# A graph layer pair on one core: node rows load behind the small weights, the count's pieces come in a row, the second chunk's weights move a step forward, and the source key is counted in strided pieces

## What is computed

```python
h = jnp.maximum(_layernorm(x, axis=-1), 0.0)
hid = silu(edge_attr_16 @ (Wfc1 / 4.0))                 # per edge
w = hid @ (Wfc2 / 8.0)                                  # per edge, 192 values
e0, e1 = f0[src], f1[src]                               # features of the source node
mid = products of w, e0, e1 and edge_attr_4
n = segment_sum(mid, dst) / max(count(dst), 1)          # mean at the destination
x = x + (self connection of h) + alpha * (n @ Wl2)
```

## Time and profile before

| | us |
|---|---|
| median of 3 runs | 9377.47 (9372.29 to 9378.21) |
| the profiled execution | 9408.31 |
| its span, first to last instruction | 9406.5 |
| first scatter of the counting stage begins | 51.09 |
| last one ends | 2201.92 |

### The profile page before, as it was taken

How to read it: one execution, slowest core, us unless ns; L and a number is a source line. 1 busy time by engine, 2 the same in 40 slices (tenths; PEclk the granted TensorE clock), 3 DMA queues, 4 the chain that set the end, 5 groups by cost and what they waited for, 6 DMA issues and landing times. The chain is left out here.

```text
span 9406.5 us, 172851 instructions
## 1 busy us (share of the span) xinstructions
PE 6619.1 (70%) x31166; PEld 4409.1 (47%) x31166; DVE 7124.6 (76%) x21336; ACT 4949.5 (53%) x16490; POOL 6802.1 (72%) x6877
## 2 busy tenths in 40 slices
PE   6666665654655555556566556778799999999999
PEld 4333333332222222222222222356588888888888
DVE  7666666665777777777777778977799999999995
ACT  4444444443444444444444445644477777777774
POOL 6777777777777777777777776456677777777770
PEclk7655556666888888888888888989899999999999
DMA  3222222225666676666676666545556666666667
GB/s 110 91 92 92 92 91 92 91 90 164 215 214 212 215 213 212 214 210 215 211 215 210 215 212 206 181 145 173 157 164 169 169 168 169 169 169 166 169 166 229
DMA packets 1189746, 1589.22 MB, mean 169 GB/s; under 512 B 452520, under 2 KB 967336, under 8 KB 1189544
## 3 DMA queue, kind: packets, MB, share of 16 engines
q1 hardware_dynamic: 789336, 836.46, 28.9%
q0 software_dynamic: 328704, 651.74, 24.0%
q10 hardware_dynamic: 71632, 100.24, 3.0%
HBM read 999.62 MB, written 1050.39 MB: 218 GB/s over the span
## 5 line engine op out<-in xcount | busy, mean ns | idle before, releaser
L1693 PE MATMUL pair<-prod_m,hot_m 128*128 128x160 f32 x14848 | 2244.5, 304 | 165.4 <-DVE prod_m L1899 128.9
L1580 POOL DMA_INDIRECT feat_m<-feat_tab,rows_m x1856 | 1830.6, 986 | 580.0 <-issue 445.4
L1693 PEld LDWEIGHTS pair<-prod_m,hot_m 128*128 128x128 f32 x14848 | 2042.9, 190 | 367.1 <-issue 365.1
L1714 ACT ACTIVATE hot_m<-hot_m,rows_m 128x128 f32<-128x128 f32 x5568 | 1728.5, 389 | 701.0 <-DVE hot_m L1882 696.7
L1591 POOL DMA_INDIRECT fetched_m<-feat_tab,index_m x1664 | 1666.4, 1001 | 517.9 <-issue 500.3
L679 POOL DMA_INDIRECT sorted_rows<-rows_e,place_e x1664 | 1629.5, 979 | 531.1 <-issue 515.3
L1726 ACT ACTIVATE prod_m<-part_m,rows_m 128x64 f32<-128x64 f32 x5568 | 1432.4, 337 | 1008.6 <-DVE part_m L1919 835.7
L1608 POOL DMA_INDIRECT sorted_rows<-later_m,place_m x1248 | 1240.8, 994 | 523.4 <-issue 376.4
L1674 PE MATMUL bank<-prod_m,hot_m 128*128 128x449 f32 x2476 | 1120.4, 576 | 548.9 <-DVE prod_m L1939 336.8
L1899 DVE TENSOR_TENSOR prod_m<-rows_m,feat_m 128x192 f32<-128x192 f32 (+2 forms) x4640 | 1284.8, 309 | 0.0
L490 PE MATMUL pair<-fc,hT_m 64*128 64x224 f32 x2496 | 397.9, 447 | 963.9 <-ACT later_m L1769 960.0
(11 more groups left out here) (259 smaller groups left out, 10631.1 us busy)
## 6 DMA issues: line engine op xcount, KB each, us to landing
agg_tab<-acc_m ACTq DMA_DIRECT2D x928, 320.0 KB
rows_m<-sorted_rows SPq DMA_DIRECT2D x928, 229.0 KB
agg_tab<-acc_m ACTq DMA_DIRECT2D x928, 224.5 KB
rows_m<-sorted_rows SPq DMA_DIRECT2D x928, 197.0 KB
feat_m<-feat_sorted SPq DMA_DIRECT2D x928, 160.0 KB
feat_sorted<-fetched_m SPq DMA_DIRECT2D x208, 640.0 KB
turned_m<-in_turned ACTq DMA_DIRECT2D x159, 256.0 KB
agg_s<-agg_tab SPq DMA_DIRECT2D x98, 320.0 KB
```

The lines of the kernel that those rows point to most:

```text
L1580: pool.indirect_dma_start(out=feat[s % RING][:, k, :], out_offset=None, in_=g.feat_tab[l.n], in_offset=bass.IndirectOffsetOnAxis(ap=rows[s ...
L1693: mm = pe.matmul(dst, hot[s % l.hot_bufs][:, k, q, :], rhs, start=(k == 0 and q < 2), stop=(k == ST_TILES - 1), skip_group_check=True)
L1714: ins = act.activation(hot[s % l.hot_bufs][:, k, 1 + q, :], hot[s % l.hot_bufs][:, k, 0, :], ACT.Copy, scale=rows[s % HELD][:, k, l.sh_at ...
```

## The change

It has five parts.

1. SyncE loads `neg_cross` before the node rows, and waits for the eight second-layer weights (`s_fc0`, issued by ScalarE) before it issues the node rows and all that follows. Chunk 2's inputs, the source key and the first 28 of the `placed` loads are issued before the loop, and the others three per step in steps 3 to 11.
2. VectorE scales the weights and copies chunk 0's fields first, and then does the six pieces of key 0 in a row; the third digit, the one-hot and the rest follow them. GpSimd's last iota waits for the digits in place of the pieces.
3. TensorE computes chunk 1's weights at the end of step 1 and ScalarE evicts them in step 1, in place of step 2. The placing stays in step 2.
4. Key 1 is counted in eight pieces of 208 columns, in steps 4 to 11 (`late_piece`, `late_sums`), with its digits in step 3 and `bin_counts(1)` in step 13. The one-hots are laid out column by column: a comparison writes one element every 13 (or 8), and the two masks for this layout are made at the start.
5. `turns` unrolls four rounds (16 steps) for these engines.

```diff
-LATE_AT = {2: (0, 1), 3: (2,), 4: (3,), 5: (4,), 6: (5,)}
+LATE_DIGITS, LATE_STARTS = 3, 13
+LATE = 208
+LATE_AT = {step: step - 4 for step in range(4, 12)}
+FIRST_OUT, OUT_STEP = 28, 3
...
+        late_hi, late_lo = ([hot[:, :, :, :].rearrange("p g v k -> p (g v k)")[:, 0:LATE * n].rearrange(
+            "p (c v) -> p c v", v=n) for hot in hots] for hots, n in ((hot_hi, NHI), (hot_lo, NLO)))
...
             load_meta(1, 1)
+            sp.dma_start(g.neg_cross[:, :], t["L1_gnn_W_out_v"][96:128, :]).then_inc(s_neg, 16)
+            sp.wait_ge(s_fc0, 16 * len(fc2[0]))
             sp.dma_start(g.x_sb[:, :, :], t["x"].rearrange("p (n d) -> p n d", d=D)).then_inc(s_in, 16)
...
+            sp.wait_ge(hid_ready, 1)
+            load_turned(2, 0)
+            sp.wait_ge(copied, 1)
+            load_meta(2, 0)
             sp.dma_start(keys[1], t["src"]).then_inc(s_key[1], 16)
-            sp.dma_start(g.neg_cross[:, :], t["L1_gnn_W_out_v"][96:128, :]).then_inc(s_neg, 16)
+            sp.wait_ge(s_neg, 17)
+            for dst, src in placed[:FIRST_OUT]:
+                sp.dma_start(dst, src).then_inc(s_w, 16)
...
-                if step is not None and 2 <= step < 8:
-                    sp.wait_ge(s_neg, 17)
-                    for dst, src in placed[(step - 2) * per_step:(step - 1) * per_step]:
+                if step is not None and 3 <= step < 12:
+                    at = FIRST_OUT + (step - 3) * OUT_STEP
+                    for dst, src in placed[at:at + OUT_STEP]:
                         sp.dma_start(dst, src).then_inc(s_w, 16)
...
+                if step is not None and step == 1:
+                    evict(1, 0, 1)
+                if step is None or step >= 3:
+                    behind(evict)(step, it, s)
                 if step is None or step >= 2:
-                    behind(evict)(step, it, s)
                     behind(to_place)(step, it, s)
...
+            def late_piece(j):
+
+                dve.wait_ge(piece_used, NPIECE + j - 1)
+                dve.wait_ge(digit, DIGITS + 4)
+                for hot, from_, count in ((late_hi, digit_hi, NHI), (late_lo, digit_lo, NLO)):
+                    for v in range(count):
+                        last = dve.tensor_scalar(hot[j % 2][:, :, v], from_[:, j * LATE:(j + 1) * LATE],
+                                                 float(v), None, ALU.is_equal)
+                last.then_inc(piece_hot, 1)
...
+            for by_k, by_h, order in ((mask_k, mask_h, "h k"), (late_mask_k, late_mask_h, "k h")):
...
             dve.wait_ge(s_key[0], 16)
             digits(0, (0, 1))
-            piece(0, 0)
             dve.wait_ge(s_fc0, 16 * len(fc2[0]))
             scale_w2(L0)
-            piece(0, 1)
             copy_meta(0, 0, 0)
+            for j in range(NPIECE):
+                piece(j)
             digits(0, (2,))
-            piece(0, 2)
...
+            def late_sums(j):
+                pe.wait_ge(piece_hot, NPIECE + j + 1)
+                for q in range(LATE // CHUNK_TILES):
+                    cols = slice(q * CHUNK_TILES, (q + 1) * CHUNK_TILES)
+                    mm = pe.matmul(bins[1], late_hi[j % 2][:, cols, :].rearrange("p k h -> p (k h)"),
+                                   late_lo[j % 2][:, cols, :].rearrange("p k l -> p (k l)"), start=False, stop=True,
+                                   skip_group_check=True)
+                mm.then_inc(piece_used, 1)
...
-                if step is None or step >= 2:
+                if step is None or step >= 3:
                     behind(weights)(step, it, s)
...
+                if step is not None and step == 1:
+                    weights(1, 0, 1)
```

More of the change, by code:

```diff
@@ L78 @@
 assert PER_TURN % 2 == 0 and MID % 2 == 0 and NBLK + BLOCK_LAG <= MID_STEPS + 2 and NCHUNK % SLOTS == 0
+assert len(LATE_AT) * LATE == NCOL and LATE <= PIECE and max(LATE_AT) + 1 < LATE_STARTS
 assert NHI * NLO >= NBIN and sum(PIECES) == NCOL and not any(n % CHUNK_TILES for n in PIECES)
@@ L131, with turns @@
     _l.sh_at, _l.key_at, _l.idx_at, _l.width = _l.wnum, _l.wnum + 3, _l.wnum + 4, _l.wnum + 5
-def turns(eng, steps, slots, body, tail=0, upto=None):
+def turns(eng, steps, slots, body, tail=0, upto=None, head=2):
     assert steps % slots == 0
     end = steps // slots if upto is None else upto
-    for it in range(2):
+    for it in range(head):
         for s in range(slots):
             body(it * slots + s, it, s)
-    with eng.Fori(2, end) as it:
+    with eng.Fori(head, end) as it:
         for s in range(slots):
@@ L885, in step_ @@
                     in_partition(step, it, c)
+                if step is not None and step == LATE_DIGITS:
+                    dve.wait_ge(s_key[1], 16)
+                    digits(1, (0, 1, 2))
                 if step is not None and step in LATE_AT:
-                    if step == min(LATE_AT):
-                        dve.wait_ge(s_key[1], 16)
-                        digits(1, (0, 1, 2))
-                    for j in LATE_AT[step]:
-                        piece(1, j)
-                if step is not None and step == 7:
+                    late_piece(LATE_AT[step])
+                if step is not None and step == LATE_STARTS:
                     dve.wait_ge(r.rank_ready, c + 1)
@@ L907, in _ @@
             bin_hot(nc, dve, r, g, 0, 0, None)
-            piece(0, 3)
             in_partition(0, 0, 0)
-            piece(0, 4)
             dve.wait_ge(s_attr, 16)
@@ L913, in _ @@
                 dve.tensor_scalar(g.attr_s[:, k, :], attr[:, :], c, None, ALU.mult).then_inc(s_scaled, 1)
-            piece(0, 5)
-            dve.wait_ge(masks, 2)
+            dve.wait_ge(masks, 4)
             bin_counts(0)
@@ L996, in step_ @@
                     if step is not None and step - 1 in LATE_AT:
-                        for j in LATE_AT[step - 1]:
-                            piece_sums(1, j)
+                        late_sums(LATE_AT[step - 1])
                     count_up(pe, r, s % 2, g.lower_bf).then_inc(r.rank_ready, 1)
@@ L1018, in _ @@
             for j in range(NPIECE):
-                piece_sums(0, j)
+                piece_sums(j)
             starts(0)
```

65 lines of the change are left out of this document (34 added, 31 removed).

## The result

| | us |
|---|---|
| the kernel after, median of 6 runs | 9416.36 (9404.39 to 9419.89) |
| the kernel before, median of 6 runs | 9377.84 (9365.1 to 9390.7) |
| ratio | 1.0039, 95% interval 1.0026 to 1.0052 |
| profiled execution of after, and its span | 9414.70, 9413.0 |
| first scatter begins, last one ends | 43.69, 2243.29 |

The change makes the kernel 38.5 us slower, 24 to 49 us by the interval. The forecast was +2.4 us and the range ended at 9400. In the profiles the last scatter ends 41.4 us later than before, 2243.29 against 2201.92; the next stage's first transfer of GpSimd also starts 41.4 us later, at 2252.40 in place of 2211.04.

A forecast was written before the change was run, and what follows sets the result against it. GpSimd's scatter issue was taken to bound the counting stage. Losses of 7.0 + 24.3 = 31.3 us against 22.2 gave +9.1, with the start's -6.7 +2.4 us: 9379.9; range 9354 to 9400.

The forecast's parts named there:

- The bound: Counting stage: GpSimd's scatters bound it, it loses time only near the start, and any change passes on one to one.
- The start: Up to the first scatter: no wait for second-layer weights, key 0's pieces in a row; first scatter at 44.4, -6.7 us.
- Rival E: Start: some load comes late and replaces the removed wait, +3 to +6 us on each case, 9385; chance 0.03.
- The next chunks: Chunks 1 and 2: 5.5 us idle stays before chunk 1, chunk 2's 5.25 goes; 7.0 us lost before the pieces.
- The digits: Key 1's digits, moved to step 3 beside scatters: taken to cost GpSimd 1 us for all, bounds 0 and 3.
- the price of the strided operation: Late pieces on VectorE: 176 to 243 ns per 208-column comparison, 3.7 to 5.1 us a piece, 4.4 taken.
- The share of 0.69: Late pieces: share of their length that GpSimd loses, kept from before's five long pieces; 8 x 4.4 x 0.69 = 24.3 us.
- B: Late pieces: one port and no block, 6.0 us a piece, VectorE bounds steps 4 to 11; 9370, chance 0.12.
- C: Late pieces: short and not blocked, scatters get in between operations; 9356, or 9362 at 5.1 us a piece; chance 0.24.
- D: Late pieces: stepping write so dear that VectorE becomes the bound; 9392 to 9413; chance 0.11 above, 0.08 below its point.
- D's upper sum of 9413: Late pieces at 546 ns an operation, 11.5 us a piece: 65 us lost, +36 us, VectorE the bound.
- D's upper part: Late pieces: the costlier end of VectorE as bound, not wholly inside the range; decides slower from 9.3 us a piece.

The follow-up runs named there:

- e6: The changed kernel with key 1's count as before the change, keeping the new load order, key 0's pieces in a row and chunk 1's earlier weights: 0.9981 of before.
- e5: The changed kernel plus nine groups of eight VectorE comparisons, priced while GpSimd has nothing to do; profile only, last scatter ends at 2278.65 us.
- e3: The changed kernel with each late piece's 21 comparisons made as two-source operations, one source in PSUM, written to the same places: 1.0097 of before.
- e2: The changed kernel with only the layout of the late one-hots undone, so each comparison writes runs of eight neighbours: 0.9994 of before.

## Why the prediction failed, point by point

- **The bound** was right. All of the loss is GpSimd's, ahead of scatter 201, and it is passed on: 46.7 us there, 41.4 us at the next stage's begin (the two differ by the 5 us of spread in before's later part), 38.5 us in the median.
- **The start**: forecast -6.7, measured -7.2 to -7.4 (first scatter) and -7.0 to -7.2 at scatter 201 by e6 alone. Rival E didn't come.
- **The next chunks**: 5.55 us idle before chunk 1, so 5.25 lost where the sum had 5.5; none before chunk 2 (forecast). The digits cost 3 x 0.86 = 2.6 us, not 1, inside the bounds of 0 to 3.
- **The step that failed is the price of the strided operation.** I put 176 to 243 ns between bounds of 68 + 208 x 0.52 and the same plus half the extra of a stepping read. It is 435 ns at a step of 13, (78.50 - 72.84) / 13, and 460 at 8. "The stepping rows of the same kind keep their rate" was the wrong choice of nearest row: that row wrote four-byte elements, and e5 shows that these keep the rate at a step of 13 too, while lone half words don't. With 9.33 us and my own share of 0.69 the pieces would have lost 51.5 us and the total been +30: whether two or four bytes are written alone was the question that decided the size.
- **The share of 0.69** was the second, smaller error: 69.4 / (8 x 9.33) = 0.93. I had taken it as an average over pieces, one of which happened to hold nothing. For one piece that holds, before's own rows gave (4.07 - 0.96) / 3.28 = 0.95. With both terms as measured the sum is 5.25 + 2.6 + 0.5 + 69.4 - 22.2 - 7.4 = +48, against 46.7 at scatter 201.
- **The rivals were cut wrongly.** B and C fell with the first piece: eight pieces of eight hold a scatter. D had the price (443 ns is the point from which it decides) but had GpSimd waiting for VectorE and not held by it. The kernel pays D's price and keeps the block, a combination that I hadn't priced: 8 x 8.7 = 69 us. That D's upper sum of 9413 lies near the measured 9416 is luck: it came from pieces of 11.5 us and idle time behind the placing, and after has neither. e3 shows D's mechanism, at twice its price; e2 shows the forecast's, the block of a cheap piece, with 2.66 us where the forecast had 4.4. By the rule of the Trainium skill, page "VectorE: DVE Perf Modes", section "What auto-detection actually checks", a stepping output doesn't end the two-port mode; the trace agrees, with eight held scatters of eight. The Trainium skill, page "Vector Engine (DVE) Microarchitecture Reference", section "Measured stream behaviour on trn2", had led to an estimate of 354 to 520 ns; the trace has 435 to 460. But its figures are for four-byte words, which cost nothing extra in e5 at a step of 13 (0.52 ns a column), so the number agrees and the cause does not. I had set the two side by side as exclusive cases and put neither price into the sum.
- **The range** left out D's upper part with a chance of 0.08. That was too little for a price that no row showed, where the nearest rows differ in the size of the element.

## What to carry to other kernels

A run of short two-port operations on VectorE can stop an indirect transfer of GpSimd for the whole length of the run (32 pieces of 32 with 208 columns, but not every one with 320), so count its price on GpSimd as the run's length once per run; ask of each such run whether one longer operation with a source in PSUM can do it, or whether it can be broken by a real wait. Do not write two-byte elements singly at steps of 8 or 13 elements, and price steps of 2 and 4 as well: change the layout so that a write has neighbours, or let one operation write the whole block. When the nearest row for an unknown price differs in element size, take the wide bound into the sum and price it together with the other mechanisms.

## What the hardware showed beyond this

- Two-byte writes in e5: 123, 177, 230, 460, 451 ns for 208 columns at steps of 1, 2, 4, 8, 13 elements; with two sources, one in PSUM, 281 and 900 ns at 1 and 13. Four-byte ones at 13 go at 0.52 ns a column.
- A scatter stands still over 21 two-port operations of VectorE, and over one-port copies between them (9.45 us), and gets through when VectorE waits (1.7 us). In before and e6 some runs let scatters through all the same, at 0.96 to 1.04 us.
- A comparison with both sources in SBUF that begins 20 to 70 ns ahead of a scatter costs it 0.25 us, one that begins 10 to 70 ns behind costs nothing. A shift of some 60 ns is worth 6 to 10 us here.
